# Attention exponentials over three PSUM banks at a time in place of two

## The reference

```python
xh = x.reshape(B, T, H, hd)                       # B=16, T=512, H=16 heads, hd=8
x_centered = xh - jnp.mean(xh, axis=1, keepdims=True)
corr = jnp.einsum('bthd,bThd->bhtT', x_centered, x_centered)
corr = jax.nn.softmax(corr, axis=-1)
out = jnp.einsum('bhtT,bThd->bthd', corr, xh)
...
x = x + 0.5 * ffn(layernorm(x))      # 8 experts, the 2 best of each token
x = x + attn(layernorm(x))
x = x + 0.5 * ffn(layernorm(x))
```

## Time and profile before

| | |
|---|---|
| median of 3 runs | 1033.71 us (1032.74 to 1034.66) |
| the profiled execution | span 1033.0 us, 20557 instructions; mean granted TensorE clock 0.991, 1.00 in both attention stages |
| busy, share of the span | PE 96%, DVE 78%, ACT 82%, POOL 49% |
| attention stages | about 197 to 349 us and 444 to 771 us |

### The profile page before, as it was taken

How to read it: one execution, slowest core, us unless ns; L and a number is a source line. 1 busy time by engine, 2 the same in 40 slices (tenths; PEclk the granted TensorE clock), 3 DMA queues, 4 the chain that set the end, 5 groups by cost and what they waited for, 6 DMA issues and landing times.

```text
span 1033.0 us, 20557 instructions
## 1 busy us (share of the span) xinstructions
PE 995.5 (96%) x6626; PEld 569.4 (55%) x6626; DVE 810.4 (78%) x2226; ACT 848.6 (82%) x1240; POOL 511.1 (49%) x602
## 2 busy tenths in 40 slices
PE   7999999999999999999999999999999999999996
PEld 5677777533332588833233333333328887777775
DVE  6899999867667677757778778777638876999898
ACT  4655553699999999889999999999998997666654
POOL 5546777744344100035776767775311000688775
PEclk8999999999999999999999999999999999999999
DMA  5533223000051244310111111112413462343442
GB/s 187 186 128 134 103 101 105 14 18 20 19 161 47 75 143 145 112 57 30 37 37 37 37 38 34 40 37 79 132 56 130 127 236 91 119 144 139 149 158 83
DMA packets 58894, 96.19 MB, mean 93 GB/s; under 512 B 8699, under 2 KB 29987, under 8 KB 58787
## 3 DMA queue, kind: packets, MB, share of 16 engines
q1 hardware_dynamic: 47664, 73.63, 21.3%
q0 software_dynamic: 9728, 19.94, 6.4%
q10 hardware_dynamic: 1396, 1.30, 0.4%
HBM read 58.46 MB, written 36.39 MB: 92 GB/s over the span
## 4 chain that ended last, share of the span: by engine, by line
PE 56%; ACT 20%; issue 11%; DVE 8%; DMA 2%; POOL 1%; SPq 0%; ACTq 0%; DVEq 0%; POOLq 0%
ACT probs L1922 13%; PE ps L1696 9%; ACT sums L1922 6%; PE ps L1681 5%; PE ps L677 3%; PE ps L693 3%; PE ps L678 3%; PE ps L679 3%; PE ps L698 3%; PE ps L694 3%; DVE low L947 3%; PE ps L1314 2%; PE ps L1316 2%; PE ps L1315 2%; PE ps L1325 2%
## 5 line engine op out<-in xcount | busy, mean ns | idle before, releaser
L1922 ACT ACTIVATE probs<-ps 128x1024 f32<-128x1024 f32 x344 | 337.2, 1144 | 6.3 <-PE ps L1681 5.2
L1637 POOL DMA_INDIRECT found<-tiles,home x152 | 152.0, 1000 | 270.8 <-DMA tiles<-sums 207.0
L1625 POOL DMA_INDIRECT sorted<-xn,slot x152 | 152.3, 1002 | 125.6 <-ACT probs L1922 76.9
L1125 ACT ACTIVATE high<-ps 128x512 fp32r<-128x512 f32 x208 | 121.0, 594 | 85.9 <-PE ps L679 82.5
L1696 PE MATMUL ps<-probs,value 128*32 128x512 f32 x1376 | 183.3, 604 | 1.8 <-ACT probs L1922 1.6
L1922 ACT ACTIVATE sums<-ps 128x1024 f32<-128x1024 f32 x168 | 175.1, 1144 | 1.6 <-PE ps L1696 0.6
L1681 PE MATMUL ps<-shared 32*128 32x512 f16 x1024 | 140.9, 384 | 8.9 <-ACT probs L1922 2.4
L947 DVE SCALAR_TENSOR_TENSOR low<-ps,high 128x512 fp32r<-128x512 f32 x208 | 133.1, 681 | 10.4 <-ACT high L1125 9.8
L1201 POOL TENSOR_TENSOR sums<-sums 128x512 f32<-128x512 f32 x70 | 90.5, 1293 | 55.8 <-DVE sums L981 47.0
L1681 PEld LDWEIGHTS ps<-shared 32*128 32x128 f16 x1024 | 38.0, 91 | 136.3 <-ACT probs L1922 73.5
L693 PE MATMUL ps<-high,weights 128*128 128x512 f32 x208 | 84.0, 404 | 6.5 <-DVE sums L981 6.4
(11 more groups left out here) (202 smaller groups left out, 1871.0 us busy)
## 6 DMA issues: line engine op xcount, KB each, us to landing
probs<-gates SPq DMA_DIRECT2D x28, 512.0 KB, 3.9
found<-sorted SPq DMA_DIRECT2D x52, 256.0 KB, 2.6
tiles<-sums SPq DMA_DIRECT2D x52, 256.0 KB, 2.0
wide<-gates SPq DMA_DIRECT2D x24, 512.0 KB, 6.0
sorted<-zeros SPq DMA_DIRECT2D x16, 512.0 KB
out<-X SPq DMA_DIRECT2D x15, 256.0 KB
sorted<-xn,slot POOLq DMA_INDIRECT x152, 2.3
found<-tiles,home POOLq DMA_INDIRECT x152
```

The costliest lines, as they stand in the source:

```text
L1125: nc.scalar.activation(high[:, third(m), c, :], ps[:, hidden_bank(m, c), :], ACT.Relu).then_inc(sm["f_high"], 1)
L1625: nc.gpsimd.indirect_dma_start(sorted_rows[group_of(q)], bass.IndirectOffsetOnAxis(ap=slot[:, q % XNS, k, j:j + 1], axis=0), xn[:, rows_sl ...
L1637: nc.gpsimd.indirect_dma_start(found[:, q % 2, k, j, :], None, tile_rows[group_of(q)], bass.IndirectOffsetOnAxis(ap=home[:, q, k, j:j + 1] ...
L1922: nc.scalar.activation(ring[ring_at(n)], ps[:, score_banks(n), :], ACT.Exp, scale=SCORE).then_inc(sm["a_probs"], 1)
```

## The change

One exponential now covers three banks. Banks 0 to 5 are two triples. The same 12 blocks of SBUF are four places of three blocks, now one tensor (`blocks`). Each stage begins with an exponential over two blocks, as 320 and 704 blocks leave two over; `EXPS` lists the first block and number of blocks of every exponential (107 and 235 of them), `EXP_OF` the exponential of every block, `exps_until(b)` how many cover all blocks before b. Triples cut across units and groups: of four exponentials, three finish a unit.

TensorE's queue is written again: in step x come the scores of exponential x+2 (which wait for exponential x), then the unit that exponential x completed, then that unit's jobs (`attn_jobs`: the former ones at their former places). The exponential waits for the values' multiplication of all units in its place. The waits at the seams are moved to the new numbers, and the banks of the expert stages with them; POOL's sends count exponentials by `exps_until_unit`.

```diff
-RING = 6
+SECOND = 5
+BANKS = 3
+RING = 4
+BLOCKS = J * Q
...
+def spans(a, b):
+
+    n, at = (b - a) % BANKS, a
+    made = [(a, n)] if n else []
+    return made + [(c, BANKS) for c in range(a + n, b, BANKS)]
...
+EXPS = spans(0, PAUSE * BLOCKS) + spans(PAUSE * BLOCKS, S * G * BLOCKS)
+EXP_OF = [x for x, (at, n) in enumerate(EXPS) for _ in range(n)]
+ENDS = EXP_OF[PAUSE * BLOCKS - 1] + 1, len(EXPS)
...
+        blocks = sb("blocks", [P, RING * BANKS, T])
+        probs = blocks[:, 0:8, :].rearrange("p (r o) t -> p r o t", o=2)
+        sums = blocks[:, 8:12, :].rearrange("p (r o) t -> p r o t", o=2)
...
+        def score_bank(x, k):
+            return BANKS * (local(x) % 2) + BANKS - EXPS[x][1] + k
...
         def tile_turn(t):
-            return 2 * tile_pair(tiles_of(t), 0)
+            return earlier_banks(tiles_of(t))
...
                 if t == a:
-                    pe.wait_ge(sm["a_probs"], (PAUSE if a == 0 else S * G) * UNITS - 2)
+                    pe.wait_ge(sm["a_probs"], ENDS[tiles_of(t)] - 1)
...
-                    if t in (a, a + 1):
-                        pe.wait_ge(sm["a_probs"], (PAUSE if a == 0 else S * G) * UNITS - 1 + t - a)
+                    if t == a + 1:
+                        pe.wait_ge(sm["a_probs"], ENDS[tiles_of(t)])
...
-        def attn_scores(pe, n):
-            g, j, half = n // UNITS, n % UNITS // 2, n % 2
-            if n % UNITS == 0:
-                pe.wait_ge(sm["a_operands"], g + 1)
-            if n == 2:
+        def attn_scores(pe, x):
+
+            first, n = EXPS[x]
+            for g in range(S * G):
+                if first <= g * BLOCKS < first + n:
+                    pe.wait_ge(sm["a_operands"], g + 1)
+            if x == 1:
+                pe.wait_ge(sm["f_scaled"], WHOLE * E - 1)
+            if x == 2:
                 pe.wait_ge(sm["f_scaled"], WHOLE * E)
...
-            reached(pe, sm["a_probs"], n - 2)
-            for odd in range(2):
-                q = 2 * half + odd
+            reached(pe, sm["a_probs"], x - 1)
+            for k in range(n):
+                g, j, q = (first + k) // BLOCKS, (first + k) % BLOCKS // Q, (first + k) % Q
                 at = slice(q * W, (q + 1) * W)
-                ins = nc.tensor.matmul(ps[:, score_banks(n).start + odd, :], kq[at, g % 2, 0, j * P:(j + 1) * P], kq[at, g % 2, 1, :],
+                ins = nc.tensor.matmul(ps[:, score_bank(x, k), :], kq[at, g % 2, 0, j * P:(j + 1) * P], kq[at, g % 2, 1, :],
                                        start=True, stop=True)
...
-            pe.wait_ge(sm["a_probs"], g * UNITS + 2 * j + 2)
+            first = g * BLOCKS + j * Q
+            pe.wait_ge(sm["a_probs"], exps_until(first + Q))
...
         def attn_tensor(pe, a, b):
...
+            end = ENDS[1] if b == S * G else ENDS[0]
+            m = a * J
+            for x in range(exps_until(a * BLOCKS), end - 1):
+                if x + 2 < end:
+                    attn_scores(pe, x + 2)
+                if x == exps_until(a * BLOCKS):
+                    attn_jobs(pe, a, 2 * m)
+                    attn_jobs(pe, a, 2 * m + 1)
+                while m < b * J - 1 and exps_until((m + 1) * Q) <= x + 1:
+                    attn_mix(pe, m // J, m % J)
+                    m += 1
+                    attn_jobs(pe, a, 2 * m)
+                    attn_jobs(pe, a, 2 * m + 1)
...
+            for x in range(exps_until(a * BLOCKS), exps_until(b * BLOCKS)):
+                first, n = EXPS[x]
+                act.wait_ge(sm["a_scores"], x + 1)
+                if x == 2:
                     act.wait_ge(sm["f_back"], WHOLE)
-                if n == PAUSE * UNITS + 4:
+                if x == ENDS[0] + 2:
                     act.wait_ge(sm["t_back"], TILE0[1])
-                if n == PAUSE * UNITS + 5:
+                if x == ENDS[0] + 3:
                     tiles_stored(act, TILE0[1])
-                reached(act, sm["a_mixed"], max((n - RING) // 2 + 1, PAUSE * J if n >= PAUSE * UNITS else 0))
-                nc.scalar.activation(ring[ring_at(n)], ps[:, score_banks(n), :], ACT.Exp, scale=SCORE).then_inc(sm["a_probs"], 1)
...
+                if local(x) >= RING:
+                    before = EXPS[x - RING]
+                    act.wait_ge(sm["a_mixed"], (before[0] + before[1] - 1) // Q + 1)
+                elif x >= ENDS[0]:
+                    act.wait_ge(sm["a_mixed"], PAUSE * J)
+                nc.scalar.activation(blocks[:, ring_at(x, 0):ring_at(x, n), :], ps[:, score_banks(x), :], ACT.Exp,
+                                     scale=SCORE).then_inc(sm["a_probs"], 1)
...
-                    pool.wait_ge(sm["a_probs"], first + PACE[i])
+                    pool.wait_ge(sm["a_probs"], exps_until_unit(first + PACE[i]))
```

More of the change, by code:

```diff
@@ L180, in before_in_slot, with exps_until, exps_until_unit, local @@
     return max([k for k in range(q) if rows_slot(k) == rows_slot(q)], default=None)
+def spans(a, b):
[5 more added lines that the diff above has]
+ENDS = EXP_OF[PAUSE * BLOCKS - 1] + 1, len(EXPS)
+def exps_until(block):
+    return EXP_OF[block - 1] + 1 if block > 0 else 0
+def exps_until_unit(n):
+    return exps_until(n * Q // 2)
+def local(x):
+    return x if x < ENDS[0] else x - ENDS[0]
 def third(m):
@@ new lines, in attn_jobs @@
+        def attn_jobs(pe, a, n):
+            g, k = n // UNITS, n % UNITS
+            s, hg = g // G, g % G
+            job, earlier = job_at(s), job_at(s - 1)
+            if n == 2:
+                ffn_back(pe, WHOLE - 1)
+            if k == (4 if g == 0 else 0) and g + 1 < S * G:
+                if g == 0:
+                    pe.wait_ge(sm["f_added"], WHOLE)
+                reached(pe, sm["a_normed"], (g - 1) // SIDES)
+                if hg == 0 and earlier is not None:
+                    pe.wait_ge(sm["r_pos"], earlier + 1)
+                if hg == 1 and job is not None:
+                    pe.wait_ge(sm["r_xnT"], job + 1)
+                if hg == 2 and job is not None:
+                    pe.wait_ge(sm["r_lg"], job + 1)
+                elif hg == 2 and s + 1 < S:
+                    pe.wait_ge(sm["a_cent"], s + 2)
+                attn_turn(pe, g + 1)
+            if k == 2 and hg == 0 and s in LAST:
+                pe.wait_ge(sm["a_operands"], g + 2)
+                group_base(pe, LAST.index(s))
+            if k == 2 and hg == 0 and s in RUSH:
+                pe.wait_ge(sm["a_operands"], g + 2)
+                group_total(pe, RUSH.index(s))
+            if k == 4 and g % SIDES == 0 and g > a:
+                if g + 1 < S * G:
+                    pe.wait_ge(sm["a_operands"], g + 2)
+                if hg == 0 and s in LAST:
+                    pe.wait_ge(sm["g_zrowf"], LAST.index(s) + 1)
+                if hg == 0 and s in RUSH:
+                    pe.wait_ge(sm["g_count"], RUSH.index(s) + 1)
+                attn_back(pe, g // SIDES - 1)
+            if k == 4 and hg == 1 and s + 1 < S:
+                pe.wait_ge(sm["a_operands"], g + 2)
+                attn_means(pe, s + 1)
+            if k == 6 and hg == 0 and job is not None:
+                pe.wait_ge(sm["a_operands"], g + 2)
+                reached(pe, sm["a_normed"], g // SIDES)
+                route_turn(pe, job)
+            if k == 6 and hg == 1 and job is not None:
+                pe.wait_ge(sm["a_cent"], s + 2)
+                route_logits(pe, job)
+            if k == 6 and hg == 3 and job is not None:
+                pe.wait_ge(sm["a_operands"], g + 2)
+                route_counts(pe, job)
@@ L2018, in first_stream @@
                 if i == TILE0[1] - 1:
[L2019 to L2020 removed]
+                    attn_scores(pe, ENDS[0])
+                    attn_scores(pe, ENDS[0] + 1)
             def second_stream(i):
```

115 lines of the change are left out of this document (30 added, 85 removed).

## The result

The changed kernel is slower. The first comparison gave a median of 1048.12 us (4 runs) against 1034.18 us; the ratio is 1.0129, 95% interval 1.0112 to 1.0145. The forecast was 1044.8 us, in a range of 1036 to 1055.

The account below looks back on a forecast made before the run. ScalarE was taken as the bound by a narrow margin, with TensorE close behind. Terms 8.8 - 0.5 + 1.0 + 0.9 + 0.9 = +11.1 us on 1033.0, plus 0.7 for the median, gave 1044.8 us, range 1036 to 1055.

Parts of the forecast that it names:

- The pace: ScalarE's exponentials over three banks: ends 1.345 us apart outside stalls, gaining 0.65 us on each of 16 laps.
- nothing saved: Three-bank exponentials at 1.375 us, as long as pairs per block: a walked lap of 30.57 us; slower case, chance 0.16.
- The allowance and the lap: Scores may start 0.80 us after an exponential's end, 1.29 before; a lap (one sequence, 64 blocks) takes 30.26 us.
- The other point of the walk: Stepping through TensorE's queue, adding up lateness and stalls, for the kernel before: a lap of 29.63 us.
- my 8.8 on fourteen laps: The fourteen attention laps with routing jobs: +0.63 us each from stalls, +8.8 us in all.
- The laps without routing: The fifth and last laps, without routing jobs: few stalls on either side, -0.5 us together.
- on neither side: Wait of the routing means on TensorE for VectorE, 0.09 us a lap, left out for both kernels.
- The start of stage one: Third exponential waits for the last dense sequence's turn back; 8 blocks done at 204.5 us, not 203.4: +1.0 us.
- The start of stage two: Wait for the stored tiles comes ahead of the fourth exponential, with 8 blocks done and not 10: +0.9 us.
- The ends of the stages: First tile's copy on ScalarE starts 0.36 us after the last exponential's end: +0.45 us, twice, +0.9 in all.
- stalls behind the runs of jobs: ScalarE gaps released by scores, 1.4 to 1.5 us a lap, just behind neighbouring turns and behind the routing logits.
- TensorE would wait far less than 30 us in 200 for ScalarE: Sign in the new trace's attention laps: TensorE's waits for ScalarE fall far below the 30.7 us in 200 seen before.

Follow-up runs that it names:

- two-pairs run: Kernel before with two pairs of banks for scores in place of three, all else the same: 1101.44 us, ratio 1.0652.
- the extra work: Routing logits multiplied once more ahead of the counts in each routed sequence: 1040.27 us on the kernel before, 1055.48 us on the changed kernel.
- split run: Changed kernel with each three-bank exponential issued as two instructions, of two banks and of one: 1062.77 us, ratio 1.0261.
- the moved wait: Changed kernel with stage one's wait for the last dense sequence's turn back put one exponential later: 1047.31 us, ratio 1.0100.
- the pairs in the new queue: Changed kernel's queue, memory and seams, but mostly two-bank exponentials in three pairs of banks, one wait an exponential later: ratio 1.0006 against the kernel before.

## Why the prediction was right

**The pace.** 1.345 us for three blocks; measured 1.345. Its other end, nothing saved, is out: an instruction costs 0.065. That is a little more than the about 51 ns that the Trainium skill gives for ScalarE on PSUM (Perfetto Trace Analysis, Optimizing Scalar/DVE Operations).

**The allowance and the lap.** 30.26 us was walked, 30.24 measured. The other point of the walk, 29.63 for the kernel before, was 0.07 low, so +0.54 came out where I had +0.63: 1.3 us of my 8.8 on fourteen laps. What the two-pairs run and the extra work gave (33.81 for 33.7; 30.94 for 30.9; 30.05 for 29.9) puts the mechanism beyond the one case: how late TensorE may be, and how jobs add up against that, sets the lap. The same section of the Trainium skill says that where ScalarE isn't saturated but makes bubbles on other engines, breaking its instructions up may let work finish sooner. The traces agree in this sense: in the same queue, pairs give a lap of 29.63 us and triples 30.24. But breaking them up without giving the banks back sooner only costs (31.08 in the split run).

**The laps without routing.** I had -0.5 for two; measured +0.48 and -0.03. So the fifth lap costs nearly as much as one that routes. The trace shows where most of it goes:

```profile
340.60 0.46 PE L1681 MATMUL ps<-summed,ones 128*128 128x128 f32 x2 [1.03 <-DVE summed L1827]
...
341.43 6.82 ACT L1979 ACTIVATE blocks<-ps 128x1536 f32<-128x1536 f32 x5 [0.61 <-PE ps L1724]
```

The means waited 1.03 us for VectorE, and the next exponential ends 0.72 us over the pace. In the kernel before the means of this lap waited 0.61 us, and 0.23 were lost. That is the wait that the prediction adds "on neither side"; with the smaller allowance it costs 0.49 more. The last lap has no means. No run isolates this. The term was mis-sized by 0.95.

**The start of stage one.** The wait cost what I walked: without the slow clock (0.86 on the unit, 0.46 on the turn back) the lag is 0.9 us, for 1.0; the run with the extra work, whose clock didn't fall, has 0.9 outright, and its 8 blocks are done 7.5 us after the first exponential's start, as walked (196.97 to 204.5). The clock I had not seen: I put the scores ahead of the unit in the walk, left TensorE idle for 1.9 us by that, and took 1.00 for the next unit all the same. The term is 2.2 in the first trace of the changed kernel and 5.2 in the second.

**The start of stage two.** +0.9 was wrong; the traces have 5.29 us before and 5.11 after, from the first exponential's end to 12 blocks. I had fixed the wait for the stored tiles at the time that one trace had. The store is issued at 445.69 there and lands 3.3 us after; the exponential starts at 449.08, 3.39 after the issue. In the changed kernel the store lands after 2.0 us and the exponential starts 2.06 after the issue, which is also when its scores are there:

```profile
454.15 0.32 SPq L475 DMA_DIRECT2D tiles<-blocks  x1
...
456.21 5.48 ACT L1979 ACTIVATE blocks<-ps 128x1536 f32<-128x1536 f32 x4 [0.53 <-PE ps L1724]
```

In the two kernels with extra work the store lands after 2.0 us in both. There the sixth exponential of the one before follows the fifth without a gap and the 12 blocks take 4.58, and those of the changed one 4.84. At an equal landing the change costs 0.3 to 0.5 here, for 0.9.

**The ends of the stages.** The copy of the first tile was to start 0.36 after the last exponential's end; it starts 0.40 after (353.82 + 2.83 = 356.65):

```profile
353.82 2.83 ACT L1979 ACTIVATE blocks<-ps 128x1536 f32<-128x1536 f32 x2
...
356.35 0.66 PE L1337 MATMUL ps<-K,found 128*128 128x128 f32 x4
...
357.05 0.60 ACT L1622 ACTIVATE xh<-ps 128x512 fp32r<-128x512 f32 x1 [0.40 <-PE ps L1337]
```

Between the stages 0.4 us remain of it. After stage two no cost shows: 262.1 and 261.6 us.

**What I named as signs.** Right: the pace, the lap, and stalls behind the runs of jobs. Wrong: that TensorE would wait far less than 30 us in 200 for ScalarE. From 500 to 700 it waits:

```profile
PEld ps L1724 <- ACT blocks L1979: 42.2, 57, 1.3
```

I had compared with 30.7, which is only the part in `probs` (another 14.3 were at `sums`, 45.0 in all), and more than that, I had thought of waiting as something that moves from one engine to the other. TensorE waits nearly as much as before, 42.2 against 45.0 us, and ScalarE waits too: with too few buffers both do, by turns.

**The sum.** By terms: 7.6 for the fourteen laps (8.8 forecast), +0.45 (-0.5), 2.2 (1.0), 0 (0.9), 0.4 (0.9): 10.6 against 11.1, and 10.5 in the trace. Four of the five terms were off by about a microsecond, two each way, and they cancelled. So the mechanism was right, in its main term to 1.2 of 8.8 us, but that the sum of the terms met the trace within 0.6 us was luck. The medians lie 11.4 and 13.9 us above the kernel before, where the trace gives 10.5; stretches at the lower clock, at the start of stage one and around 30 us, are the likeliest reason for the rest, which no run here isolates.

## What to carry to other kernels

An instruction that covers more of a fixed set of buffers also holds more of it at once. Before making one longer, work out how late the producer may be (the free time from a buffer's release to its next need, less the two engines' latencies), and walk the producer's queue for neighbouring side jobs that add up to more; an average of its work won't show it. Use the long form where the queue is thin and the short one where jobs crowd; here that was worth 0.09 us a lap over pairs alone.

When a change moves a wait ahead of other work in TensorE's queue, look at what stood in the gap: the gap can cost more than its length, if the clock falls after it, as it did in six of seven traces here.

## What the runs showed of the hardware

Seven traces have an idle gap of 1.9 us on TensorE ahead of the first unit, after 160 us at full clock in which it was busy for all but 2 to 3 us. In six of them the clock then fell to the 1.2 GHz level: for 3.41 us in four (the first run of the changed kernel, the one with the moved wait, the pairs in the new queue, triples only where few jobs stand), for 13.65 in two (the second run of the changed kernel, the split one). In the seventh, the changed kernel with extra work, it didn't fall. So the same kernel can lose much, little or nothing here. The kernel before, with the first unit in that gap, kept its clock there in both traces (its own and the one with extra work). With two pairs of banks it lost it for 3.41 us from 207.69, so this gap isn't the only way to it. Filled with matmuls of zeros, the gap went by without a fall, in both kernels that had them.

A store of 256 KB that is waited for landed 2.0 us after its issue in one run and 3.3 in another, so a wait for one should stand in a sum with a range.
